# A decoder layer on one core: another order of the small steps within a slot of the attention pipeline

## What is computed

```python
x = layernorm(x + retention(x))      # scores * decay mask, no softmax; norm of the output, gate sigmoid(x Wg + bg), Wo
x = layernorm(x + cross(x, ctx))     # softmax attention against ctx
x = layernorm(x + ffn(x))            # causal softmax attention, layernorm, then a mixture of 8 experts, top 2, gelu, 512 wide
```

## Time and profile before

| what | value |
| --- | --- |
| median of 3 runs | 1430.68 us (1429.87 to 1431.65) |
| the profiled execution | 1430.61 us |
| its span from first to last instruction | 1429.3 us |
| busy: TensorE | 1083.5 us (76%) |
| busy: VectorE | 930.3 us (65%) |
| busy: ScalarE | 798.2 us (56%) |
| busy: GpSimd | 1012.3 us (71%) |

### The profile page before, as it was taken

One profiled execution on the slowest core, in us unless ns is written; L12 is line 12 of the kernel. 1 busy time (PEld: TensorE's weight loads), 2 busy tenths in 40 slices (PEclk: granted clock), 3 DMA queues, 4 the chain that ended last, 5 costly groups with the idle time before them and its releaser, 6 DMA issues. The chain is left out here.

```text
span 1429.3 us, 45221 instructions
## 1 busy us (share of the span) xinstructions
PE 1083.5 (76%) x17314; PEld 758.0 (53%) x17314; DVE 930.3 (65%) x2328; ACT 798.2 (56%) x1768; POOL 1012.3 (71%) x1032
## 2 busy tenths in 40 slices
PE   5877777778888888899888888741888988888440
PEld 2544444445555555555554455531878887778100
DVE  3677677786666667668888989642444455445685
ACT  2233333368887888788665665310555555545255
POOL 2677777775666665555677878875787888878698
PEclk9677777777777778899988988655999999999655
DMA  4344221212232232222212122111222222221353
GB/s 112 84 131 117 85 62 51 62 47 61 63 86 80 79 86 63 66 67 55 62 49 69 58 62 64 36 44 53 63 74 66 69 72 71 72 68 54 110 149 102
DMA packets 136018, 104.37 MB, mean 73 GB/s; under 512 B 19307, under 2 KB 130412, under 8 KB 135772
## 3 DMA queue, kind: packets, MB, share of 16 engines
q1 hardware_dynamic: 127388, 84.10, 21.5%
q0 software_dynamic: 8416, 17.38, 3.6%
HBM read 37.38 MB, written 26.75 MB: 45 GB/s over the span
## 5 line engine op out<-in xcount | busy, mean ns | idle before, releaser
L719 POOL TENSOR_TENSOR Plo<-P 128x1024 f16<-128x1024 f32 x192 | 363.7, 1894 | 251.4 <-ACT P L680 174.2
L1087 ACT ACTIVATE G<-bank,we 128x128 f32<-128x128 f32 x540 | 154.1, 368 | 143.9 <-PE bank L1064 143.9
L1114 POOL DMA_INDIRECT expert_rows<-yo,ix x135 | 170.9, 1266 | 42.1 <-POOL ix L1108 23.5
L465 PE MATMUL bank<-Vh,P 64*128 64x17 f16 (+1 forms) x3072 | 141.3, 171 | 69.5 <-POOL Plo L719 69.2
L1064 PE MATMUL bank<-hTb,we 128*128 128x128 f32 x1080 | 153.6, 287 | 44.1 <-issue 28.0
L465 PEld LDWEIGHTS bank<-Vh,P 64*128 64x128 bf16 x3072 | 124.2, 96 | 95.4 <-issue 47.0
L769 DVE TENSOR_REDUCE mx<-bank 128x16 f16<-128x1024 f32 x128 | 156.9, 1226 | 16.2 <-PE bank L422 14.0
L1096 DVE COPY we<-wx 128x1156 f32 x135 | 122.2, 905 | 68.6 <-DVE yo L1102 61.1
L1064 PEld LDWEIGHTS bank<-hTb,we 128*128 128x128 f32 x1080 | 135.0, 196 | 58.8 <-issue 36.2
L641 ACT ACTIVATE Kz<-kh,col 128x512 f16<-128x512 f16 x256 | 163.1, 713 | 0.1
L737 POOL DMA_INDIRECT block_rows<-xs,slots x128 | 130.0, 1016 | 37.1 <-issue 34.7
(11 more groups left out here) (159 smaller groups left out, 2391.2 us busy)
## 6 DMA issues: line engine op xcount, KB each, us to landing
Qz<-qh SPq DMA_DIRECT2D x192, 64.0 KB
Kst<-kh SPq DMA_DIRECT2D x192, 64.0 KB, 2.0
xrow<-block_rows SPq DMA_DIRECT2D x135, 65.0 KB
y_t<-expert_rows SPq DMA_DIRECT2D x16, 512.0 KB, 4.1
Qz<-ql SPq DMA_DIRECT2D x96, 64.0 KB
Kst<-kl SPq DMA_DIRECT2D x96, 64.0 KB, 2.0
xs<-x SPq DMA_DIRECT2D x16, 256.0 KB, 3.4
cg<-ctxt SPq DMA_DIRECT2D x16, 256.0 KB, 3.1
```

The lines of the kernel that those rows point to most:

```text
L465: pe.matmul(o, up[rows_b, cs], Vh[g % 3][rows_b, t, c, 0:nv], start=True, stop=False)
L719: pool.tensor_tensor(Plo[n % 2][:, :], P32[n % 2][:, :], upper(n), ALU.subtract).then_inc(f_Pl.of(n), 1)
L1087: i = act.activation(G[b][:, c, :], bank[:, 2 + p, c * P:(c + 1) * P], ACT.Gelu_apprx_tanh, bias=we[b][:, B1 + c:B1 + c + 1])
L1114: pool.indirect_dma_start(ydst[:, :], bass.IndirectOffsetOnAxis(ix2[s % 4][:, :], 0), yo[s % 2][:, :], None).then_inc(b_sc.of(s), 16)
```

## The change

Only the order of steps within the slots changes; no step is added or removed.

- VectorE (`dve_slot`): the row maxima come first in a slot. In k0 of retention the bias of V is added (new function `dve_value_sums`), then P is decayed, then Vl is made; before, V32 and Vl both came ahead of P. In k0 of cross and self the maxima come ahead of Vl, and in k3 ahead of the residual. The decayed P comes ahead of kl (k2) and of ql (k3), and behind the residual.
- ScalarE (`act_slot`): norm 1 of group g - 6 moves from k0, behind the exp, to k2, where it comes behind the gate of k1, kh, the exp and the four key blocks. In k0 stays norm 1 of the first self groups' turn (`last(g - 5)`).
- GpSimd (`pool_slot`): the rescale of norm 0 comes ahead of the low part in k3. The bias add on x comes last in k1, behind the low part and the rescale of norm 1; before, it was first.
- SyncE (`sp_slot`): the store of x2 moves from k1 of g to k0 of g + 1.

```diff
@@ sp_slot
-        if k == 1 and begun(g - 6):
-            sp_store(g - 6)
+        if k == 0 and begun(g - 7):
+            sp_store(g - 7)
@@ act_slot
-        if k == 0 and begun(g - 6) and not last(g - 6):
+        if k == (0 if last(g - 5) else 2) and begun(g - 6) and not last(g - 6):
             act_normalise(1, g - 6, tiles_of(g - 6)).then_inc(f_y.of(g - 6), 1)
@@ pool_slot
-        if k == 1 and begun(g) and kind(g) != "self":
-            pool.wait_ge(*f_xT(g))
-            pool.tensor_tensor(tiles_of(g), tiles_of(g), brow("a_bo" if kind(g) == "ret" else "x_bo"), ALU.add).then_inc(f_xb.of(g), 1)
...
         if k == 0 and last(g - 5):
             pool_rescale(1, g - 5)
+        if k == 3 and begun(g - 3) and kind(g - 3) == "ret":
+            pool_rescale(0, g - 3)
         if 0 <= s - LT < TILES:
             pool_low(s - LT)
-        if k == 3 and begun(g - 3) and kind(g - 3) == "ret":
-            pool_rescale(0, g - 3)
         if k == 1 and begun(g - 5) and not last(g - 5):
             pool_rescale(1, g - 5)
+        if k == 1 and begun(g) and kind(g) != "self":
+            pool.wait_ge(*f_xT(g))
+            pool.tensor_tensor(tiles_of(g), tiles_of(g), brow("a_bo" if kind(g) == "ret" else "x_bo"), ALU.add).then_inc(f_xb.of(g), 1)
@@ dve_values, split in two
+    def dve_value_sums(g):
         if kind(g) == "ret":
             dve.wait_ge(*f_V(g))
             dve.tensor_tensor(V32[:, :].rearrange("p (t d) -> p t d", d=P), bankB.rearrange("p (t d) -> p t d", d=P), brow("a_bv"),
                               ALU.add).then_inc(f_V32.of(g), 1)
-            v = V32[:, :]
+
+    def dve_values(g):
+        vh = Vh[g % 3][:, :, :, 0:2 * DH].rearrange("p t c e -> p (t c) e")
+        v = V32[:, :] if kind(g) == "ret" else bankB
         dve.wait_ge(*f_Vh(g))
@@ dve_slot
+        if NG * GT <= s - LS < TILES:
+            dve_maxima(s - LS)
+        if k == 0 and begun(g - 1):
+            dve_value_sums(g - 1)
+        if k == 3 and begun(g - 4):
+            dve_residual(g - 4)
+        if 0 <= s - LT < NG * GT:
+            dve_decayed(s - LT)
         if k == 0 and begun(g - 1):
             dve_values(g - 1)
-        if k == 3 and begun(g - 4):
-            dve_residual(g - 4)
-        if NG * GT <= s - LS < TILES:
-            dve_maxima(s - LS)
         if k == 3 and begun(g):
             dve_low(g, f_qh, l_Q(g - 2), ql, qh, {"ret": "a_bq", "cross": "x_bq", "self": "k_zero"}[kind(g)], f_ql)
         if k == 2 and begun(g):
             dve_low(g, f_kh, l_K(g - 2), kl, kh, {"ret": "a_bk", "cross": "x_bk", "self": "k_zero"}[kind(g)], f_kl)
-        if 0 <= s - LT < NG * GT:
-            dve_decayed(s - LT)
```

More of the change, by code:

```diff
@@ L776, in dve_low @@
                                  op0=ALU.add, op1=ALU.subtract).then_inc(done.of(g), 1)
-    def dve_values(g):
-        vh = Vh[g % 3][:, :, :, 0:2 * DH].rearrange("p t c e -> p (t c) e")
-        v = bankB
+    def dve_value_sums(g):
         if kind(g) == "ret":
```

## The result

The changed kernel takes 1443.88 us (median of 5, 1440.90 to 1448.21) against 1430.68 (also 5, 1427.07 to 1432.28): **ratio 1.0098, 95% interval 1.0074 to 1.0122**. The forecast was 1437 in a range of 1421 to 1460. The profiled execution took 1443.58 us with a span of 1442.3, 13.0 more than before.

What follows compares the result with a forecast made beforehand. Rings of waits between engines were taken to set 18.2 us a retention and 17.1 us a cross group; -6 + 10.5 + 4 - 2 = +6.5 us on a 1429.3 span gave 1435.8, so 1437 us, range 1421 to 1460.

Steps and rivals of the forecast that it cites:

- Norm 1 in the gapless part of cross: Cross, ScalarE k2: norm 1 ahead of qh costs 1.55 us less credits, net +0.75 a group, +10.5 us over fourteen.
- The 0.25 us credited for the wait of qh: Cross, ScalarE: qh waits 0.40 us for its projection in one period, nothing in another; 0.25 us credited against the norm.
- The credit of 0.5 for the maxima: Cross, VectorE: maxima ahead of Vl fill idle time and shorten TensorE's 2.03 us stop; 0.5 us a group credited.
- The first self groups: First five self groups still have a cross norm at k2: another +4 us.
- the ring that follows: Retention: GpSimd's low part, rescale, bias add and gate product, then output projection, become late; 17.7 against 18.2 us a group.
- The bounds of -20 and +12: Retention: range around the -6 us forecast for twelve groups at 0.5 us a group.
- (a) to (e): Retention: rescale ahead of low part (2.1 us), norm 1 behind gate (1.55), P ahead of kl (0.7), ql (0.7), Vl (1.1).
- The port: Retention: Vl starts about 0.1 us ahead of GpSimd's k0 low part and keeps the shared SBUF port, lasting 0.7 us.
- Rival A: Retention: Vl loses the port and lasts over 2 us; about 19.5 us a group, +16 us, 1459 in all; chance 0.22.
- Rival B: Cross: halved stop at maxima's turn raises TensorE's clock, returning about 1 us a group over some 16; 1421; chance 0.22.
- Rivals C and D: C: retention -0.8, cross +0.5 a group, about 1431, chance 0.13; D: nine routing choices beat low part, 1.5 us each, 1424, 0.05.
- The routed groups: Self stage: GpSimd's low parts hold up routing choice and scaling, so maxima first changes little; -2 us (+2 to -14).

Runs made afterwards that it cites:

- first pair: The changed kernel against the kernel before, as first measured, on a chip inferred to be another than the experiments'; 1443.88 against 1430.68 us, ratio 1.0098.
- e1: Changed kernel with norm 1 back in k0 from the cross stage on, retention keeping it in k2; 1436.25 for 1452.95 us, ratio 0.9880.
- e2: Kernel before with only norm 1 moved to k2 and the store of x2 with it; 1482.28 us, ratio 1.0209.
- e3: Changed kernel with the maxima last again, behind Vl in k0 and behind residual and decayed P in k3; 1478.74 us, ratio 1.0181.
- e10: Kernel before with VectorE's new order alone; one run, 1430.06 us beside 1459.70.
- a1: Changed kernel unaltered, run again on the experiments' chips; 1463.90 for 1456.84 us, ratio 1.0051.
- b1: Kernel before unaltered, profiled again on an experiments' chip; profile span 1461.4 us.
- e5: Changed kernel with the maxima behind Vl and the residual in the self stage alone; 1470.27 us, ratio 1.0078.
- e7: Kernel before with only GpSimd's rescale of norm 0 put ahead of the k3 low part; one run, 1453.45 us beside 1458.21.
- e4: Changed kernel with GpSimd's bias add first in k1 again; 1447.64 us, ratio 0.9941.
- e8: Changed kernel with Vl of retention behind the results of k0, so it starts in the middle of a low part; one run, 1474.10 us beside 1458.21.
- e6: Changed kernel with norm 1 back in k0 from cross on and GpSimd's bias add first in k1; 1429.05 us, ratio 0.9809.

## Why the prediction was right, and where not

- **Norm 1 in the gapless part of cross: right, and a little too cheap.** Forecast +0.75 us a group, measured +1.0 (first pair) and +0.93; e1 takes it away again. The terms as written give 0.80, not 0.75 (1.55 less 0.25 less 0.5). The 0.25 us credited for the wait of qh did not come back: moved alone the block costs its full 1.55 (e2). The credit of 0.5 for the maxima is 0.55 (e3) and 0.48 alone (e10). 1.55 less 0.55 is the 1.0 that was measured. Forecast for fourteen groups +10.5, measured +13.9 and +13.0.
- **The first self groups**: +4 forecast, +6.0 measured in the first pair; a1 has +0.7 against b1, whose own stretch is 5 us longer than in the first profile (clock 0.87 for 0.94). Two terms lie under it, of which the forecast had one. The norm costs 6.9 there (e2) and the maxima in front give 7.5 (e5), which was put at nearly nothing ("maxima first changes little").
- **Retention: right in sign and in the ring that follows.** Forecast 17.7 us a group, measured 17.5; forecast -6 us up to the cross stage, measured -11.7. The wait that was named as next, of the output projection for the gate product, went from 0.86 to 2.29 and is 2.0 to 3.6 us in nine of ten groups, and the lower clock just behind it is there (2.05 and 1.75 us). Mis-sized were two terms: the ten full groups gained 0.74 us each and not 0.5, and the groups before the sixth gained 4.3 us that I had not counted. The bounds of -20 and +12 do not follow from the ring's 15.5 to 19.5 us, which over twelve groups are -32 and +16. The clock of the ten groups rose from 0.74 to 0.81 in the first pair and to 0.77 in a1; their length came out the same (174.9 and 174.4).
- **What the ring made of the edits.** I listed (a) to (e) as gains on one ring and took the new ring as their common floor. e7 and e10 show that floor from the other side: the rescale alone gives 9 us, VectorE's part alone 11, both with the norm and the bias add 7.6. The bias add last costs 6.1 of it (e4). Without it the edits give 13.7.
- **The port: right.** Vl started first and kept the port, as at 665.28, and not as at 750.21. Rival A is refuted: Vl takes 0.68 us in every full period. e8 shows that the later of the two waits all the same. "SBUF — State Buffer" of the Trainium skill, section "SBUF: two separate sides", says so, and this trace agrees where GpSimd was idle before: 0.68 and 2.27 us.
- **Rival B, the clock pays back, is refuted for this change.** The stop at the maxima's turn halved, but the key projection ran at the upper level (1.12 us) in none of the thirteen cross groups read, before or after, and the clock of cross is 0.77 for 0.79. Where norm 1 is back in k0 the clock is 0.80 (e1) and 0.83 (e6) and a few key projections take 1.12 (four and three of thirteen). But e3, with the maxima last, has three as well, so the halved stop is not shown to be what does it.
- **Rivals C and D did not come.** The two stages did not cancel, and all eight scalings by g1 that met a low part in the changed kernel's routed groups lost the port (2.79 to 3.03 us).
- **The routed groups: the term that failed.** Forecast -2 us, measured +6.9. In the first pair the changed kernel's last six routed periods are 23.7 to 23.9 us, the kernel before has 22.2 to 23.7. The rows of the two stretches, before and after:

```profile
650.60:870.00 219.40, 189.66 (x3411) 115.07 (x3412) 187.87 (x426) 143.94 (x230) 157.86 (x145) 0.88 0.22 62
659.00:885.30 226.30, 198.63 (x3411) 121.56 (x3410) 191.68 (x425) 144.13 (x230) 157.66 (x144) 0.84 0.21 60
```

For the same 3411 products TensorE is busy 9.0 us longer, at a granted clock of 0.84 for 0.88. A lower clock thus goes with the +6.9, and no such term stands in the forecast; whether the clock is the cause or follows from new stops is not shown. Nothing in the experiments reproduces the +6.9, since on their chips something else fills these groups and they scatter by 7 us. Its cause stays open.
- **How near the sum came is partly luck.** Against their forecasts, retention came out 5.7 us lower and what lies behind the attention 2.3 lower; cross came out 3.4 higher, the first self groups 2.0, the two groups between the stages 0.3 and the routed groups 8.9. These add up to 6.6 us, what the measured span of 1442.3 lies above the forecast 1435.8 but for rounding.

## What to carry to other kernels

An engine may be idle for a fifth of a period and still have a part of the period without a gap: here a block of 1.65 us, 1.55 from start to start, cost 1.55 us a group when it moved into that part alone (e2), and moving it out again gave 0.98 (e1) or 1.46 (e6 against e4). So ask of a moved step not how busy its engine is but in which half of the ring it lands, and of a list of reorderings which one stands directly ahead of the next wait: here two of five edits (norm 1 in cross, the bias add) turned a version that is 1.9% faster than the kernel before (e6) into one that is 0.5% slower on the same chip (a1).

## What the runs showed of the hardware

**TensorE stops within a tile's sums, on some chips.** In the first two profiles the 48 products of a tile take 0.6 us in every tile of the routed groups but one (0.97). In each of the twelve profiles of the experiments they take 1.0 to 3.4 us in 25 to 33 of some 40 tiles, from the first indirect transfer of GpSimd's queue to the end of the attention. The first such tile starts about 1 us behind that transfer in all twelve, though the transfer comes anywhere from 660 to 725 us. Ahead of it only one to three tiles of retention are stretched, in some profiles; the changed kernel's first profile has one such, a stop of 1.14 us at 95.76. The products of the kernel before on such a chip (b1) with TensorE's next step, and two of the weight loads between them:

```profile
747.74 0.19 PE L465 MATMUL bank<-Vh,P 64*128 64x17 f16 x2
...
749.69 1.16 PE L580 MATMUL bank<-W,xT 128*128 128x128 f32 x8
```
```profile
748.58 0.09 PEld L465 LDWEIGHTS bank<-Vh,P 64*128 64x128 bf16 x1 [0.41 <-issue]
...
749.34 0.09 PEld L467 LDWEIGHTS bank<-Vl,P 64*128 64x128 bf16 x1 [0.60 <-issue]
```

Two stops of half a us for which the trace names no releaser. The ten routed groups of the same program take 232.8 us with them and 219.4 without. That the indirect transfers are the cause wasn't tried, and the first self groups, ahead of any such stop, were already 5 us longer in b1.

**Starting first doesn't always win the port.** In the changed kernel the scaling by g1 starts 0.56 us ahead of a low part and takes 3.02 us, while Vl, 0.16 us ahead of its low part, takes 0.68. A descriptor job runs on GpSimd as the scaling starts, and GpSimd is idle as Vl starts. But the job alone does not decide it, as the same scaling in e6 shows, below:

```profile
807.42 3.02 DVE L844 TENSOR_TENSOR xs<-xs,row 128x512 f32<-128x512 f32 x1
...
807.00 0.96 POOL L737 DMA_INDIRECT block_rows<-xs,slots  x1 [0.30 <-issue]
807.98 1.91 POOL L719 TENSOR_TENSOR Plo<-P 128x1024 f16<-128x1024 f32 x1
```
```profile
745.98 0.96 POOL L737 DMA_INDIRECT block_rows<-xs,slots  x1 [0.30 <-issue]
746.63 0.68 DVE L844 TENSOR_TENSOR xs<-xs,row 128x512 f32<-128x512 f32 x1
747.03 2.02 POOL L719 TENSOR_TENSOR Plo<-P 128x1024 f16<-128x1024 f32 x1
```

The low part follows the job by 0.02 us in the first case and by 0.09 in the second. All fourteen profiles together have 105 scalings that start 0.3 to 0.7 us ahead of a low part while such a job runs. 49 of them take 2.8 to 3.0 us, and in all of these the low part starts within 0.03 us of the job's end. The other 56 take 0.68, and in all but one the low part starts 0.05 us or more behind the job. So in these traces a GpSimd instruction that follows without a gap keeps the port from VectorE, and one that has to wait even 0.05 us lets VectorE through; why is not shown.
